# Taylor attention, first part of a Trainium2 kernel: the PSUM unit of the state is placed last in its head group

## The reference, cut to what matters

```python
# branch 1 (the part that is changed): 16 heads of width 16
f(u) = [1, u / 16**0.25, u*u / (4 * 2**0.5), pairs u_i*u_j / 4]
kv = cumsum(f(k)[..., None, :] * v[..., :, None], axis=time)
y = einsum('bhtD,bhtdD->bhtd', f(q), kv)
y = y / (sum(f(q) * cumsum(f(k), axis=time), -1) + 1e-12)
attn = y @ Wo.T
# branch 2: two layers of windowed softmax attention (8 heads of 64) and a gated FFN
out = x + attn + branch2(xn)
```

## Time and profile before

| what | us |
|---|---|
| median of 3 runs | 3475.45 (3474.73 to 3481.47) |
| the profiled execution | 3475.38 |
| its span in the trace | 3473.6 |
| third sequence: four attention groups | 16.72, 14.57, 15.80, 16.11 |
| projection that follows | 38.60 |
| busy in the whole span: PE, DVE, ACT, POOL | 3330.0, 2736.3, 2518.9, 1536.3 |

### The profile page before, as it was taken

How to read it: one execution, slowest core, us unless ns; L and a number is a source line. 1 busy time by engine, 2 the same in 40 slices (tenths; PEclk the granted TensorE clock), 3 DMA queues, 4 the chain that set the end, 5 groups by cost and what they waited for, 6 DMA issues and landing times.

```text
span 3473.6 us, 96643 instructions
## 1 busy us (share of the span) xinstructions
PE 3330.0 (96%) x36960; PEld 2498.5 (72%) x36960; DVE 2736.3 (79%) x8256; ACT 2518.9 (73%) x5629; POOL 1536.3 (44%) x1547
## 2 busy tenths in 40 slices
PE   7898889887799999999999999999999999999999
PEld 4555545554588787788788788888788888888887
DVE  4767777777688888888888888888888888888886
ACT  5667776666577777777777777777777777777775
POOL 4444444444444444444444444444444444444443
PEclk9999999999899999999999999999999999999999
DMA  6756676654422222222222222222222222222211
GB/s 159 174 128 139 126 154 144 141 100 87 134 63 62 73 66 62 73 67 62 73 66 62 73 67 62 73 66 62 73 68 62 72 67 62 72 69 62 71 45 43
DMA packets 289965, 293.94 MB, mean 85 GB/s; under 512 B 40960, under 2 KB 221536, under 8 KB 288992
## 3 DMA queue, kind: packets, MB, share of 16 engines
q1 hardware_dynamic: 289504, 287.74, 34.7%
HBM read 104.89 MB, written 58.73 MB: 47 GB/s over the span
## 4 chain that ended last, share of the span: by engine, by line
PE 73%; DVE 1%; POOL 0%; ACT 0%; issue 0%; DMA 0%; SPq 0%; DVEq 0%; POOLq 0%
PE f_ps L1575 19%; PE f_ps L1683 16%; PE f_ps L1695 10%; PE f_ps L1660 6%; PE f_ps L1639 4%; PE f_ps L1580 3%; PE f_ps L1602 3%; PE f_ps L1620 3%; PE f_ps L1649 2%; PE f_ps L1609 2%; PE f_ps L1688 2%; PE f_ps L1624 2%; PE f_ps L1667 1%; PE f_ps L1561 0%; ACT pr L1491 0%
## 5 line engine op out<-in xcount | busy, mean ns | idle before, releaser
L1246 POOL TENSOR_TENSOR turned<-qk,rot 128x256 f32<-128x256 f32 x512 | 405.4, 813 | 1250.5 <-ACT qk L1458 1235.4
L1575 PE MATMUL f_ps<-wqkv_s,hT 128*128 128x512 f32 x1536 | 707.2, 596 | 8.9 <-DMA hT<-xnT_dram 5.5
L1683 PEld LDWEIGHTS f_ps<-hnT,w_s 128*128 128x128 f32 x5120 | 591.7, 192 | 63.0 <-issue 59.8
L1326 DVE CUSTOM_DVE_ANT_0 pr<-f_ps,masks_s 128x192 f32<-128x192 f32 x1024 | 326.4, 355 | 360.7 <-PE f_ps L1609 358.7
L1683 PE MATMUL f_ps<-hnT,w_s 128*128 128x128 f32 x5120 | 592.5, 275 | 2.5 <-DVE hnT L1383 2.5
L1491 ACT ACTIVATE pr<-pr,nmax,rnorm 128x192 f32<-128x192 f32 x1024 | 545.0, 535 | 44.4 <-DVE nmax L1333 44.4
L1575 PEld LDWEIGHTS f_ps<-wqkv_s,hT 128*128 128x128 f32 x1536 | 276.9, 191 | 273.6 <-issue 186.7
L1343 DVE TENSOR_SCALAR pr<-pr,rsum 128x192 f32<-128x192 f32 x1024 | 445.4, 497 | 9.0
L1695 PE MATMUL f_ps<-w_s,act_u 128*128 128x256 f32 x1536 | 352.7, 379 | 0.0
L687 ACT ACTIVATE weights<-t_ps,four_s 128x1024 f32<-128x1024 f32 x320 | 326.4, 1132 | 26.1 <-PE t_ps L843 26.1
L1253 POOL TENSOR_TENSOR rnorm<-ssq,f_mhalf 128x8 f32<-128x8 f32 x128 | 255.7, 1998 | 163.9 <-DVE ssq L1303 163.9
(11 more groups left out here) (151 smaller groups left out, 6873.5 us busy)
## 6 DMA issues: line engine op xcount, KB each, us to landing
vw<-vw SPq DMA_DIRECT2D x628, 128.0 KB, 2.5
qkT<-parts_dram SPq DMA_DIRECT2D x384, 128.0 KB, 5.7
kT<-kT SPq DMA_DIRECT2D x124, 256.0 KB, 2.7
parts_dram<-shared SPq DMA_DIRECT2D x64, 384.0 KB, 3.1
xnT_dram<-xnT SPq DMA_DIRECT2D x8, 1025.0 KB, 5.4
xs<-x_dram SPq DMA_DIRECT2D x8, 1024.0 KB, 7.4
xn_dram<-xn SPq DMA_DIRECT2D x8, 1024.0 KB, 5.0
attn_dram<-ao SPq DMA_DIRECT2D x8, 1024.0 KB, 9.6
```

The source lines that it names most:

```text
L1246: g.tensor_tensor(turned[:, heads, f], qk[:, heads, z], sines, ALU.mult).then_inc(done, 1)
L1326: last = v.tensor_tensor_reduce(out=chances(h), in0=ps[:, SCORES[p], k * 256:k * 256 + BAND], in1=mask_of(it)[:, HALF - k * HALF:HALF - k ...
L1575: last = mm(ps[:, b, :], rows, wqkv_s[:, l, c, i * INNER:(i + 1) * INNER], start=(c == 0), stop=(c == KC - 1))
L1683: last = mm(ps[:, UP[j // 2], o:o + P], w1_s[:, l, c, half * FULL + j * P:half * FULL + j * P + P], hnT[:, c, :], start=(c == 0), stop=(c ...
```

## The change

In the list of units the state moves from behind the near units to the end of its group, so it is made last and its transposes come behind the fourth near step's value product. DVE's `keep_state` and `turn_state` move behind the last mask and `add_before(g, 0)`. ACT's `linear_rows` for a group g >= 1 moves from behind the rest unit of the group before to behind the second unit of group g. The denominators of the fourth group take the way of the others: `invert` is split into `read_den` and `write_den`, the write of group 3 stands on SP behind `store_xn` and `load`, and DVE inverts and spreads it at the start of the next projection, so that `normalise` keeps only L422 and L425. `tile_stats` and `variances` of the next sequence but one move from the attention to the end of the projection, POOL's `root` to the start of its attention, and `layer_norm` is spread over all four groups, two tiles in each. The semaphores den_ready and rden_ready go. Left out of the diff below: POOL's `normalise` and PE's `turn_state` and `scores`, in which only counts and the position of the state unit follow suit.

```diff
@@ -179,11 +177,13 @@
         PIECE = SEQ // 4
+        SPREADS = 2 * (GROUPS - 1) + 1
...
         UNITS = [(kind, i, pair) for kind, i, pair in
-                 [("near", i, pair) for i in range(NS) for pair in range(2)] + [("state", NS, 0)] +
-                 [("past", NS, pair) for pair in range(2)] + [("rest", NS, 0)]]
+                 [("near", i, pair) for i in range(NS) for pair in range(2)] + [("past", NS, pair) for pair in range(2)] +
+                 [("rest", NS, 0), ("state", AS, 0)]]
         NU = len(UNITS)
+        STATE = NU - 1
...
         def squares_to(n):
@@ -217,15 +217,18 @@
             def load(b):
...
-            def invert(b, g):
-
-                i, row = b * (GROUPS - 1) + g, ONE[g % 2]
+            def read_den(b, g):
                 sp.wait_ge(yT_ready, 2 * (b * GROUPS + g) + 2)
-                sp.dma_start(den_flat[:, :], yT[row:P:VP, g, :]).then_inc(den_in, 16)
-                sp.wait_ge(den_inverse, i + 1)
+                sp.dma_start(den_flat[:, :], yT[ONE[g % 2]:P:VP, g, :]).then_inc(den_in, 16)
+
+            def write_den(b, g):
+
+                sp.wait_ge(den_inverse, b * GROUPS + g + 1)
                 if g >= 1:
-                    sp.wait_ge(y_group, i)
-                sp.dma_start(den[row:P:VP, :], den_flat[:, :]).then_inc(den_out, 16)
+                    sp.wait_ge(y_group, b * (GROUPS - 1) + g)
+                elif b >= 1:
+                    sp.wait_ge(y_ready, b * TILES)
+                sp.dma_start(den[ONE[g % 2]:P:VP, :], den_flat[:, :]).then_inc(den_out, 16)
...
             def store_xn(b):
@@ -279,11 +282,14 @@
                         load_heads(b, g + 2)
-                    invert(b, g)
+                    read_den(b, g)
+                    write_den(b, g)
+                read_den(b, GROUPS - 1)
...
                     load(b + 2)
+                write_den(b, GROUPS - 1)
@@ -348,10 +354,10 @@
             def attention(b):
+                if b + 1 < B:
+                    root(b + 1)
...
                 pairs(b, 1)
-                if b + 1 < B:
-                    root(b + 1)
@@ -393,17 +399,17 @@
             def invert_den(b, g):
-                dve.wait_ge(den_in, 16 * (b * (GROUPS - 1) + g + 1))
+                dve.wait_ge(den_in, 16 * (b * GROUPS + g + 1))
...
             def spread_den(b, g):
-                dve.wait_ge(den_out, 16 * (b * (GROUPS - 1) + g + 1))
+                dve.wait_ge(den_out, 16 * (b * GROUPS + g + 1))
...
             def keep_den(b, g):
-                dve.wait_ge(spread, 2 * (b * (GROUPS - 1) + g) + 1)
+                dve.wait_ge(spread, SPREADS * b + 2 * g + 1)
...
             def normalise(b, t):
@@ -411,14 +417,8 @@
                 if t == 0:
-                    dve.wait_ge(yT_ready, 2 * (b * GROUPS + GROUPS))
                     dve.wait_ge(y_group, b * (GROUPS - 1) + g)
-                else:
-                    dve.wait_ge(y_tile, i)
-                v.stream_shuffle(den[:, cols], yT[:, g, cols], [ONE[odd]] * 32).then_inc(den_ready, 1)
-                dve.wait_ge(den_ready, i + 1)
-                v.reciprocal(den[:, cols], den[:, cols]).then_inc(rden_ready, 1)
-                dve.wait_ge(rden_ready, i + 1)
+                    dve.wait_ge(spread, SPREADS * (b + 1))
@@ -432,18 +432,28 @@
             def project(b, last=None):
                 if last is not None:
-                    for t in range(3):
-                        normalise(last, t)
-                for m in range(BLOCKS // 2):
+                    invert_den(last, GROUPS - 1)
+                for m in range(2):
+                    subtract_high(b, m)
+                if last is not None:
+                    spread_den(last, GROUPS - 1)
+                for m in range(2, BLOCKS // 2):
...
                 if last is not None:
-                    normalise(last, 3)
+                    for t in range(3):
+                        normalise(last, t)
                 for m in range(BLOCKS // 2, BLOCKS):
+                    subtract_high(b, m)
                     if last is not None:
-                        normalise(last, m)
-                    subtract_high(b, m)
+                        normalise(last, m - 1)
+                if last is not None:
+                    normalise(last, TILES - 1)
+                if b + 1 < B:
+                    for t in range(TILES):
+                        tile_stats(b + 1, t)
+                    variances(b + 1)
...
             def attention(b, following):
                 def add_before(g, half):
@@ -468,10 +478,10 @@
                 def keep_state(g):
...
                     dve.wait_ge(state_ps, group + 1)
-                    v.tensor_copy(state_T, ps[:, unit_bank(g * NU + 2 * NS), 0:FORMS]).then_inc(state_kept, 1)
+                    v.tensor_copy(state_T, ps[:, unit_bank(g * NU + STATE), 0:FORMS]).then_inc(state_kept, 1)
...
                 def turn_state(g):
-                    group, bank = b * GROUPS + g, unit_bank(g * NU + 2 * NS) + 1
+                    group, bank = b * GROUPS + g, unit_bank(g * NU + STATE) + 1
@@ -505,29 +515,21 @@
                     mask_diagonals(g, 1)
-                    if following is not None and g <= 1:
-                        for t in range(4 * g, 4 * g + 2):
-                            tile_stats(following, t)
-                    if following is not None and g >= 2:
-                        layer_norm(following, 2 * (g - 2))
-                        layer_norm(following, 2 * (g - 2) + 1)
+                    if following is not None:
+                        layer_norm(following, 2 * g)
+                        layer_norm(following, 2 * g + 1)
...
                     mask_diagonals(g, 2)
-                    if following is not None and g <= 1:
-                        for t in range(4 * g + 2, 4 * g + 4):
-                            tile_stats(following, t)
-                    if following is not None and g == 1:
-                        variances(following)
...
                     mask_diagonals(g, 3)
+                    mask_diagonals(g, 4)
+                    add_before(g, 0)
                     keep_state(g)
-                    mask_diagonals(g, 4)
                     turn_state(g)
-                    add_before(g, 0)
@@ -535,9 +537,6 @@
                 add_before(GROUPS - 1, 1)
-                if following is not None:
-                    for t in range(TILES // 2, TILES):
-                        layer_norm(following, t)
@@ -561,6 +560,8 @@
             attention(B - 1, None)
+            invert_den(B - 1, GROUPS - 1)
+            spread_den(B - 1, GROUPS - 1)
@@ -678,8 +679,6 @@
                         a.activation(rest_w, ps[:, bank, :], ACT.Square, bias=own_s[:, P:P + 1]).then_inc(squared, 1)
-                        if n // NU + 1 < GROUPS:
-                            linear_rows(b, n // NU + 1)
@@ -688,6 +687,8 @@
                         linear_rows(b, 0)
+                    if n >= NU and n % NU == 1:
+                        linear_rows(b, n // NU)
@@ -875,14 +876,15 @@
                     kind, i, pair = UNITS[n % NU]
-                    last_of[n // NU, i] = n
+                    if kind != "state":
+                        last_of[n // NU, i] = n
...
                         attend(*ends[n - BEHIND])
-                    if n % NU == 2 * NS + 1 and n < units:
+                    if n % NU == STATE and n < units:
```

More of the change, by code:

```diff
@@ L165, in taylor_block @@
         y_pair = sem("y_pair")
-        den_ready = sem("den_ready")
-        rden_ready = sem("rden_ready")
         y_tile = sem("y_tile")
@@ L321, in normalise @@
             def normalise(b, n):
-                pool.wait_ge(spread, 2 * (b * (GROUPS - 1) + n) + 2)
+                pool.wait_ge(spread, SPREADS * b + 2 * n + 2)
                 for c in range(0, SEQ, PIECE):
@@ L805, in turn_state @@
                 def turn_state(g):
-                    bank = unit_bank(g * NU + 2 * NS) + 1
+                    bank = unit_bank(g * NU + STATE) + 1
                     pe.wait_ge(state_kept, b * GROUPS + g + 1)
@@ L823, in scores @@
                         pe.wait_ge(qkT_in[g % 2], 16 * 2 * SLOTS * (2 * b + g // 2 + 1))
-                    if b == 0 and n == 2 * NS + 1:
+                    if b == 0 and n == 2 * NS:
                         pe.wait_ge(forms_set, 1)
```

## The result

The changed kernel takes 3530.64 us in the median of four runs (3527.0 to 3539.8), the kernel before 3475.09 (four runs too, one more than in the table above): a ratio of 1.0163, 95% interval 1.014 to 1.0187. The profiled execution took 3527.0 with a span of 3525.2, so 51.6 more than before.

The account below looks back on a forecast made before the run. PE and ACT hold each other through three PSUM slots in plain groups; PE's stream bounds the projection. Terms +48.9 + 18.6 + 1.6 + 2.4 - 5.5 - 4.5 - 3.5 = +58 gave 3533 us, range 3503 to 3549.

Parts of the forecast that it names:

- The stand: Group 0, six sequences: DVE waits 9.6 us in layer_norm for the store of attn, PE restarts at low clock; +48.9 us.
- 4.6 us of the lone one: Rival: the store of attn lands in 4.6 us, DVE stands 5 us less six times, 3503 us; chance 0.05.
- Heads: Last group: later reciprocal delays load_heads(b, 3), PE waits 2.7 us in each of eight sequences; +13.6, with clock +18.6.
- 5 us of clock: After the last group's wait for heads: the clock falls in five more sequences, about 1 us each; +5.
- its 0.3: End of the last group: the product of the past step waits for turn_state, 0.3 us per sequence; +2.4.
- State last: Plain group: the wait moves from ahead of the past squares to the group boundary, ACT idle 1.4 us; +1.6.
- term of +0.8: Group 1, all eight sequences: 0.1 us per boundary from making the state last; +0.8.
- Group 0 without the stand: Group 0, first and last sequence: 14.6 us instead of 16.7, -2.7 each; -5.5 together.
- rival without any stand: Rival: the store does not hold DVE, group 0 shrinks in six more sequences, 3472 us; chance 0.06.
- Projection: Seven projections: earlier splitting takes 0.65 us off the 1.57 us wait for ACT's values; -4.5.
- likeliest case: The forecast itself, with landings of the store of 8.7 to 11.7 us: 3522 to 3546 us; chance 0.52.
- two cases without the stand: Rivals: the store does not hold DVE, 3472 us, chance 0.06; heads no later as well, 3453 us, chance 0.04.

Follow-up runs that it names:

- e1: Changed kernel with the stores of attn on a semaphore of their own, so layer_norm waits for the store of xn alone: 3482.45 us, ratio 1.0026.
- e4: Kernel before with only the state unit moved last, with keep_state, turn_state and linear_rows moved along: 3487.27 us, ratio 1.0033.
- e9: Changed kernel with a separate semaphore for stores of attn and the state unit, its copies and linear rows back in their old place: 3465.60 us, ratio 0.9977.
- e5: Changed kernel with its shared count untouched and layer_norm in groups 1 to 3 (3, 3 and 2 tiles), none in group 0: 3478.93 us, ratio 1.0014.
- e2: Changed kernel with SP issuing load_heads(b, 3) ahead of write_den(b, 0): 3543.49 us, ratio 1.0197.
- e3: Changed kernel with both a separate semaphore for stores of attn and load_heads(b, 3) issued ahead of write_den(b, 0): 3485.77 us, ratio 1.0032.

## Why the prediction was right

**The stand.** The forecast had DVE held in six sequences from 5.2 us to 14.8 us into the attention and group 0 at 24.9 us; the six groups measured 24.4 to 25.9, together +49.2 against +48.9, with landings of 9.8 in the median (9.6 in the earlier trace rows). The own count shows the cause by taking it away, the late normalisation by going around it. The clock came as priced: 0.50 in the windows after the wait, with the product at 284.15 taking 1.93 us and the same one at 300.37, at a clock of 1.00, taking 1.04. The store did not land in the 4.6 us of the lone one: of the eight in the changed kernel the shortest took 4.6 and the median 9.8, in the third sequence 8.6. By the fit in the Trainium skill, "DMA: Bandwidth & Descriptors", section "Anatomy of one DMA", 4.4 us were to be expected as an estimate. The fit is for another issue path; the last store, with no loads of heads beside it, took 4.6, and beside other transfers the measured 9.8 decides against it. The same page's section "Why a DMA increments its semaphore by 16 and not by 1" advises a semaphore for each slot in flight because a wait on a shared count can pass too early. No run here shows that; e1 shows the other side, that a shared count can also make a wait last too long: a count for each kind of store gave 48 us.

**Heads.** The write was expected 2.6 us after group 2 begins and came at 2.7 (309.75 against 307.01). The wait was as forecast, 2.87 us in the third sequence and 21.6 in eight, 2.7 each (the sum should read +13.4, not +13.6):

```profile
324.44 1.48 PE L844 MATMUL t_ps<-qkT 96*32 96x512 bf16 x24 [2.87 <-DMA qkT<-parts_dram]
```

Group 2 still cost +17.1 against +14.4, since PE's waits for DVE's masks rose there from 0.5 to 6.3 us, which the forecast had at nothing. In group 3, +4.4 against +7.1, neither part came as forecast. The 5 us of clock did not come: the clock was 0.50 for 10.2 us of group 3 before and for 9.2 after, and it fell only behind the waits for heads of the fifth to seventh sequence, though those of the second to fourth, 2.6 to 2.9 us, were as long. A single row of 1.87 us was not enough to price it. The end of attention cost more than its 0.3: PE waits there for `turn_state` (L489) for 4.9 us in seven sequences, and a group 3 at full clock takes 17.2 to 17.6 us where it took 16.7. That groups 2 and 3 together are +21.5 as forecast is luck.

**State last.** ACT's wait is 1.54 us at the boundary of groups 1 and 2 (2.0 to 2.9 at that of 0 and 1) and a plain group 14.59 to 14.60 in all eight second groups: I had 1.4 and 14.65. The step that failed is to take the third sequence's group 1 for all of them: the second groups of before ran from 14.16 to 18.96. In them PE stood 7.7 us for nothing that the trace names and 2.1 us for `turn_state` (L479), and the clock was 0.50 for 6.3 us; all of that is gone. The term of +0.8 measured -10.9. Of it, 4.4 us are the pause in the second sequence, which the stand hides (e1 has -6.6); state last alone has -4.3 (e4) and the rest of the change, with the own count, -1.1 (e9).

**Group 0 without the stand.** I gave the first and the last sequence 2.7 us each; they won 0.9 and 1.8. The step that failed is the one that followed PE and ACT there and not DVE, whose `other_rows`, with `layer_norm` to a smaller part (e5), delays the mask of step 3. The rival without any stand inherits this: it was put at 3472, and e1 has 3482.

**Projection.** -1.5 instead of -4.5: the wait for ACT's values fell from 1.57 to 0.88 as reckoned, but 0.5 us of it came back at PE's products of the output, of which 0.21 is a wait for DVE's L425 that was not there before.

The forecast of 3533 is 2.4 above the median, and its +58 is 6 above the +51.6 of the two profiled executions. The stand was foreseen as it came; that the total is so near is in part luck, since group 1 was overrated by 11.8 us and the gains in group 0 and in the projection by 3 each the other way. Its lower end for the likeliest case, 3522, does not follow from a landing of 8.7 us, which gives 3528, and its two cases without the stand have 0.06 and 0.04, not 0.05 each.

## What to carry to other kernels

Before moving an instruction earlier, look at every wait that it carries, and ask for each count which transfers are in it and when the last of them lands at the new place; a wait that never showed in a trace can hold a whole queue. Here a small transfer that an engine waits for had to go ahead of the large ones in the issue order, so its producer must be early on its own engine: moving the reciprocal up won 27 us, moving the transfers around lost 13. Two halves of a change should be timed alone: here the losing waits were worth 78 us and hid a kernel that is 0.6% faster than before.

## What the runs showed of the hardware

A 16 KB transfer issued right behind twelve of 128 KB on the same queue landed 4.6 to 7.3 us after its issue (e2 and e3, first write of each sequence), against at most 3.1 us when it went just ahead of them (changed kernel, third sequence). A 1 MB store took 4.6 us alone and 9.8 in the median of eight. After PE had stood 8 us the granted clock was 0.50 in each of six groups 0; after waits of 2.2 to 4.0 us it fell in three of seven sequences and not in the other four. And a PE pause that the trace puts down to nothing stands in group 1 of the second sequence in all nine kernels without the stand, which then takes 16.5 to 19.0 us, beside a packet of the queue of instructions; it is absent (14.6) in the three kernels with the stand, where that group begins 4 to 16 us later. What PE waits for there was not tried.
